# Input products of the second recurrence made beside attention, and one POOL power for three variances in the readout

## What is computed

```python
h = tok(x)                      # four 512x512 attentions per batch element -> (8, 512, 128)
xn = layernorm(layernorm(h)) * norm_g + norm_b
# first recurrence (reservoir), 256 wide, 512 steps, strictly one after the other
r_t = 0.95 * tanh(x_in_t + r_{t-1} @ W_res.T) + 0.05 * r_{t-1}
# second recurrence (linear)
delta = softplus(xn @ w_delta + b_delta);  a = exp(A * delta)
s_t = a_t * s_{t-1} + (xn @ W_B.T) * (1 - a_t) / A
read(s) = gelu(layernorm(s) @ W_ro.T + b_ro)        # s is 256 wide, the result 128
gate = sigmoid(layernorm(h) @ W_gate.T + b_gate)
h = h + read(r) * gate + read(s) * (1 - gate)
h = h + layernorm(h)            # the last stage only changes columns from 128 on, and there are 128
```

## Time and profile before

| | us |
|---|---|
| median of 3 runs (614.12 to 618.78) | 617.13 |
| profiled execution, its own time | 613.99 |
| its span | 612.1 |

### The profile page before, as it was taken

How to read it: one execution, slowest core, us unless ns; L and a number is a source line. 1 busy time by engine, 2 the same in 40 slices (tenths; PEclk the granted TensorE clock), 3 DMA queues, 4 the chain that set the end, 5 groups by cost and what they waited for, 6 DMA issues and landing times.

```text
span 612.1 us, 29176 instructions
## 1 busy us (share of the span) xinstructions
PE 571.5 (93%) x11514; PEld 469.6 (77%) x11514; DVE 524.4 (86%) x2325; ACT 430.7 (70%) x2258; POOL 202.6 (33%) x426
## 2 busy tenths in 40 slices
PE   6888787999999999999999999999999999999972
PEld 2555454788888888888888888888889988998862
DVE  6789886799888889899989999999767788899985
ACT  5587775477777777777777777777758677777764
POOL 1556464011000001110111111011100599898886
PEclk9999999899999999999999999999999999999997
DMA  6000000000000000000000000000020000000001
GB/s 219 2 2 1 2 2 1 3 4 4 4 3 4 3 4 3 4 4 4 4 4 4 4 3 3 4 3 4 3 73 2 3 20 17 20 16 20 16 19 31
DMA packets 8632, 8.35 MB, mean 14 GB/s; under 512 B 944, under 2 KB 7088, under 8 KB 8496
## 3 DMA queue, kind: packets, MB, share of 16 engines
q1 hardware_dynamic: 8208, 5.51, 3.0%
q10 hardware_dynamic: 288, 0.99, 0.5%
HBM read 3.35 MB, written 2.10 MB: 9 GB/s over the span
## 4 chain that ended last, share of the span: by engine, by line
PE 63%; POOL 23%; issue 9%; DVE 2%; DMA 1%; ACT 1%; POOLq 0%; SPq 0%; DVEq 0%
PE PS L1479 20%; PE PS L1529 15%; POOL prob_lo L448 4%; PE PS L1490 4%; POOL r_dev L516 4%; PE PS L1500 4%; POOL ln_small L526 3%; PE PS L1431 2%; PE PS L1438 2%; PE PS L1432 2%; PE PS L1494 2%; PE PS L1486 2%; POOL k L539 2%; POOL k L502 2%; POOL ln_small L530 2%
## 5 line engine op out<-in xcount | busy, mean ns | idle before, releaser
L637 ACT ACTIVATE y<-PS 128x16 f16<-128x16 f32 x512 | 94.3, 184 | 132.3 <-PE PS L1494 121.4
L1529 PE MATMUL PS<-ballast,ident 128*128 128x245 f16 (+7 forms) x648 | 142.7, 296 | 0.0
L1041 DVE TENSOR_TENSOR y_lo<-ys,y 128x16 f16<-128x16 f32 x512 | 96.5, 188 | 49.1 <-ACT ys L638 38.8
L1479 PE MATMUL PS<-y_lo,res_hi 128*128 128x8 f16 x2048 | 128.0, 168 | 2.3 <-DVE y_lo L1041 1.1
L1479 PE MATMUL PS<-y,res_hi 128*128 128x8 f16 x2048 | 127.4, 168 | 0.2
L1479 PEld LDWEIGHTS PS<-y,res_hi 128*128 128x128 f16 x2048 | 96.8, 96 | 38.8 <-ACT y L637 19.0
L1479 PE MATMUL PS<-y,res_lo 128*128 128x8 f16 x2048 | 123.4, 166 | 0.0
L453 POOL TENSOR_TENSOR small<-small,minus_half 128x2 f32<-128x2 f32 x32 | 25.6, 799 | 295.2 <-DVE y_lo L1041 260.3
L638 ACT ACTIVATE ys<-PS 128x16 f32<-128x16 f32 x512 | 99.1, 194 | 0.0
L640 ACT ACTIVATE kp<-PS 128x16 f32<-128x16 f32 x512 | 97.5, 190 | 0.0
L1479 PEld LDWEIGHTS PS<-y_lo,res_hi 128*128 128x128 f16 x2048 | 87.9, 96 | 5.5 <-DVE y_lo L1041 3.2
(11 more groups left out here) (240 smaller groups left out, 1483.8 us busy)
## 6 DMA issues: line engine op xcount, KB each, us to landing
ys<-in_x SPq DMA_DIRECT2D x8, 256.0 KB, 7.6
out<-gate_all SPq DMA_DIRECT2D x24, 64.0 KB, 1.5
mats<-in_mats ACTq DMA_DIRECT2D x1, 709.0 KB, 5.0
h_last<-h_all SPq DMA_DIRECT2D x4, 128.0 KB, 2.7
gate_last<-gate_all SPq DMA_DIRECT2D x4, 128.0 KB, 2.9
out<-gate_last SPq DMA_DIRECT2D x16, 32.0 KB, 1.9
rows<-in_rows ACTq DMA_DIRECT2D x1, 257.5 KB, 7.5
wall<-in_wall SPq DMA_DIRECT2D x1, 256.0 KB, 4.8
```

What stands on the lines that cost most here:

```text
L637: a_.activation(y16[:, :].rearrange("p (m b) -> p m b", m=NH), pre, ACT.Tanh, scale=back).then_inc(y16_ready, 1)
L1041: v.tensor_tensor(y_lo[:, :], ys[:, :, bass.ds(i * STEPS + (1 + t), 1)].rearrange("p n o -> p (n o)"), y16[:, :], ALU.subtract).then_inc(l ...
L1479: t_.matmul(dst[:, m, :], wts[:, k, m * P:m * P + P], st[:, k * B:k * B + B], start=False, stop=False, skip_group_check=True)
L1529: t_.matmul(at[:, 0:size], ident16[:, :], ballast[:, 0:size], start=False, stop=True, skip_group_check=True)
```

## The change

1. The 64 input products become 32 "drives", one per tile: two fp32 matmuls (m = 0, 1) into the last 256 columns of PSUM bank 7, made in the attention bodies. For tiles 0 to 10 they stand at t = 10 of bodies 4 to 14, for tiles 11 to 30 at t = 6 of bodies 4 to 23, for tile 31 at t = 15 of body 23. At these places `pads` returns after the drive, so the fillers of that step go. ACT copies each drive to SBUF (`take_drive`, 128x256) at t = 2 of the next body or t = 7 of the same, the last one at t = 0 of body 24.
2. `feed` is gone from PE in body 24 and after. DVE's `feed_scaled` and `recur` read and write the drives in SBUF, so that both their inputs are in SBUF.
3. The 112-column filler inside a step now also runs in bodies 25 to 31.
4. POOL takes read n-1's two variances and read n-3's layernorm variance with one addition and one power over three columns. It now waits for both (ACT's sums and DVE's `bn_aggr`) before the addition. L524 and L526 go, in the bodies; in the tail they stay as they were.
5. SP waits for the first 16 rows of the second recurrence before it moves the last quarter of h and gate, since the drives of the first quarter borrow that place.

```diff
+        last = sb("last", [P, NH, B, P])
+        h_last, gate_last = last[:, 0, :, :], last[:, 1, :, :]
+        drives = sb("drives", [P, NH, 2 * B + B // 2, P])
+        late_drives = mats[:, 0:B * P].rearrange("p (m k n) -> p m k n", m=NH, n=P)
+        DRIVE = MISC[:, 512 - NH * P:512]
...
+        FIRST_DRIVE = 4
+        LATE_DRIVE = FIRST_DRIVE + AHEAD - 2
+        def early_drive(i):
+            return i - FIRST_DRIVE if FIRST_DRIVE <= i < FIRST_DRIVE + LATE_DRIVE else None
+        def late_drive(i):
+            j = i + AHEAD - 2
+            return j if LATE_DRIVE <= j < NT - 1 else None
...
             sp.wait_ge(h_ready, NT)
+            sp.wait_ge(ssm_done, B * NH + EIGHT_FREE)
...
-                if 1 in active and u == 2:
-                    j = n - 1
-                    pool.wait_ge(r_squared, 2 * j + 2)
-                    g.tensor_tensor(r_var[:, :], r_ss[:, 1 - e, :], r_eps[:, :], ALU.add).then_inc(r_var_ready, 1)
-                    pool.wait_ge(r_var_ready, j + 1)
-                    pool.wait_ge(readout_scaled, j - 1 + TWO_FREE)
-                    g.tensor_tensor(r_dev[:, 1 - e, :], r_var[:, :], minus_half[:, :].to_broadcast([P, 2]), ALU.pow
-                                    ).then_inc(r_dev_ready, 1)
...
+                def deviations(cols, slot, added, made, count):
+                    g.tensor_tensor(var_three[:, cols], sums_read[:, slot, cols.start + 1:cols.stop + 1], eps_three[:, cols], ALU.add
+                                    ).then_inc(added, 1)
+                    pool.wait_ge(added, count)
+                    g.tensor_tensor(dev_three[:, slot, cols], var_three[:, cols],
+                                    minus_half[:, :].to_broadcast([P, cols.stop - cols.start]), ALU.pow).then_inc(made, 1)
...
+                joined = norm_last and not alone
+                if norm_last:
+                    if joined:
+                        pool.wait_ge(ln_stats, n - 2 + FREE)
+                    if n > 4:
+                        pool.wait_ge(r_out, n - 4)
+                if read_last:
+                    pool.wait_ge(r_squared, 2 * n)
+                    pool.wait_ge(readout_scaled, n - 2 + TWO_FREE)
+                    deviations(slice(0 if joined else 1, 3), 1 - e, r_var_ready, dev_made, n)
...
+            def take_drive(j):
+                act.wait_ge(drive_made, drive_count(j))
+                a_.activation(drives_of(j), DRIVE.rearrange("p (m n) -> p m n", m=NH), ACT.Copy).then_inc(drive_taken, 1)
...
             def feed_scaled(s, c):
-                dve.wait_ge(ssm_fed, c * 8 + s + 1)
-                fed = PS[:, 6 + s % 2, 0:P]
+                dve.wait_ge(drive_taken, drive_count(half_q(c) * B + c % 2 * 4 + s % 4))
+                fed = drive_row(s, c)
...
-                    v.tensor_tensor_scan(row, row, PS[:, 6 + s % 2, 0:P], first, ALU.mult, ALU.add).then_inc(ssm_done, 1)
+                    v.tensor_tensor_scan(row, row, fed, first, ALU.mult, ALU.add).then_inc(ssm_done, 1)
...
-                zeros = 112 if i < FIRST_DECAY else 0
+                zeros = 112 if i != FIRST_DECAY else 0
...
+            def drive(j):
+                b, q = j % B, j // B
+                pe.wait_ge(b_t_ready, 1)
+                if drive_count(j) > 1:
+                    pe.wait_ge(drive_taken, drive_count(j) - 1)
+                pe.wait_ge(xn_ready, j + 1)
+                for m in range(NH):
+                    one = t_.matmul(DRIVE[:, m * P:m * P + P], b_t[:, m * P:m * P + P], xn[:, b, 1 + q * P:1 + q * P + P],
+                                    start=True, stop=True, skip_group_check=True)
+                one.then_inc(drive_made, 1)
...
+                if t == 6 and late_drive(i) is not None:
+                    pe.wait_ge(gate_raw, late_drive(i) + 1)
+                    drive(late_drive(i))
+                    return
+                if t == 10 and early_drive(i) is not None:
+                    pe.wait_ge(gate_raw, j - 1)
+                    drive(early_drive(i))
+                    return
...
-                if t >= 4:
-                    feed((t - 4) % 8, (t - 4) // 8)
```

More of the change, by code:

```diff
@@ L174, in build @@
         sp_tmp = sb("sp_tmp", [P, 3, NT])
-        r_ss = sb("r_ss", [P, 2, 2])
+        sums_read = sb("sums_read", [P, 2, 4])
+        ln_mv, r_ss = sums_read[:, :, 0:2], sums_read[:, :, 2:4]
         r_mean = sb("r_mean", [P, 2, 2])
-        r_eps = sb("r_eps", [P, 2])
-        r_var = sb("r_var", [P, 2])
-        r_dev = sb("r_dev", [P, 2, 2])
+        eps_three = sb("eps_three", [P, 3])
+        var_three = sb("var_three", [P, 3])
+        dev_three = sb("dev_three", [P, 2, 3])
+        r_dev = dev_three[:, :, 1:3]
         ln_st = sb("ln_st", [P, 6])
-        ln_mv = sb("ln_mv", [P, 2, 2])
-        ln_small = sb("ln_small", [P, 2, 3])
+        ln_small = sb("ln_small", [P, 2, 2])
         ssm = keep[:, 0:SSM_LEN].rearrange("p (m q n) -> p m q n", m=NH, q=NQ + 1)
@@ L272, in build @@
         ssm_zeroed = sem("ssm_zeroed")
-        ssm_fed = sem("ssm_fed")
+        drive_made = sem("drive_made")
+        drive_taken = sem("drive_taken")
         ssm_scaled = sem("ssm_scaled")
@@ L339, in build, with drives_of, drive_count @@
         FED_EARLY = STEPS - 4
+        FIRST_DRIVE = 4
+        LATE_DRIVE = FIRST_DRIVE + AHEAD - 2
+        def drives_of(j):
+            q, b = j // B, j % B
+            if q == 0:
+                return last[:, :, b, :]
+            if j < NT - B // 2:
+                return drives[:, :, j - B, :]
+            return late_drives[:, :, b - B // 2, :]
+        def drive_count(j):
+            return 2 * j + 2 if j < LATE_DRIVE else 2 * (j - LATE_DRIVE) + 1 if j < 2 * LATE_DRIVE else j + 1
+        def early_drive(i):
[3 more added lines that the diff above has]
+            return j if LATE_DRIVE <= j < NT - 1 else None
         assert IN_SCAN == SPLIT
@@ new lines, in norm_scales @@
+                def norm_scales(slot):
+                    g.tensor_tensor(ln_small[:, slot, 0:1], dev_three[:, slot, 0:1], ones[:, 0:1], ALU.add)
+                    g.tensor_scalar(ln_small[:, slot, 1:2], ln_mv[:, slot, 0:1], dev_three[:, slot, 0:1], minus_one[:, :], ALU.mult, ALU.mult
+                                    ).then_inc(ln_dev_ready, 1)
+                read_last, norm_last = 1 in active and u == 2, 3 in active and u == 2
+                joined = norm_last and not alone
[4 more added lines that the diff above has]
+                        pool.wait_ge(r_out, n - 4)
@@ new lines, in readout @@
+                if read_last:
+                    pool.wait_ge(r_squared, 2 * n)
+                    pool.wait_ge(readout_scaled, n - 2 + TWO_FREE)
+                    deviations(slice(0 if joined else 1, 3), 1 - e, r_var_ready, dev_made, n)
+                if norm_last:
+                    if joined:
+                        pool.wait_ge(dev_made, n)
+                    else:
+                        pool.wait_ge(ln_stats, n - 2 + FREE)
+                        deviations(slice(0, 1), 1 - e, ln_var_ready, ln_pow_ready, n - IN_SCAN + 1)
+                        pool.wait_ge(ln_pow_ready, n - IN_SCAN + 1)
+                    norm_scales(1 - e)
@@ L693, in _ @@
                         gate_half(i)
+                    if t == 2 and early_drive(i - 1) is not None:
+                        take_drive(early_drive(i - 1))
+                    if t == 7 and late_drive(i) is not None:
+                        take_drive(late_drive(i))
                     if (t, i) == (7, 17):
@@ L747, in _ @@
                 scan(t, FIRST_DECAY, FIRST_DECAY % REGIONS)
+                if t == 0:
+                    take_drive(NT - 1)
                 if t >= 2:
@@ L1259, in ssm_row, with drive_row @@
                 return ssm[:, s // 4, half_q(c) + 1, (c % 2) * 4 * P + (s % 4) * P:(c % 2) * 4 * P + (s % 4) * P + P]
+            def drive_row(s, c):
+                return drives_of(half_q(c) * B + c % 2 * 4 + s % 4)[:, s // 4, :]
             def feed(s, c):
@@ L1529, in pad @@
                 t_.matmul(at[:, 0:size], ident16[:, :], ballast[:, 0:size], start=False, stop=True, skip_group_check=True)
+            def drive(j):
[8 more added lines that the diff above has]
+                one.then_inc(drive_made, 1)
             def pads(t, i):
                 j = i + AHEAD
+                if t == 6 and late_drive(i) is not None:
[6 more added lines that the diff above has]
+                    return
+                if t == 15 and j == NT:
+                    pe.wait_ge(gate_raw, NT)
+                    drive(NT - 1)
+                    return
                 tile, early, fill_at = j < NT, j <= NT, i % REGIONS < 2 and t in (4, 5, 8, 9)
@@ L1554, in pads @@
                         pe.wait_ge(gate_raw, j - 1)
+                        if late_drive(i) is not None:
+                            pe.wait_ge(drive_taken, drive_count(late_drive(i)))
                         for n in range(2 if fill_at else 4):
@@ L1745, in _ @@
```

(3 more changed lines are left out.)

42 lines of the change are left out of this document (10 added, 32 removed).

## The result

| | before | changed |
|---|---|---|
| median, us | 614.58 (6 runs, 613.78 to 618.78) | 640.14 (6 runs, 639.29 to 642.68) |
| span of the profiled execution | 612.1 | 640.9 |
| mean granted clock of it, share of full | 0.992 | 0.906 |

The changed kernel takes 1.0406 times the time of before, 95% interval 1.0371 to 1.0442: 25.6 us slower. The profiled execution is its slowest, 642.68, so the traces stand 28.8 us apart.

The account below looks back on a forecast made before the run. PE paced body 24; in the readout PE, DVE and POOL were nearly full, POOL's list as long as a read. Terms -2.4 + 2.2 - 0.6 + 0.8 + 2.0 = +2.0 us: median 619, range 610 to 627.

Parts of the forecast that it names:

- body 24, feeds gone: Body 24: 12 feeds leave PE, each step with a feed falling from 1.10 to 0.90 us; -2.4 us.
- drives on PE, attention bodies: Steps 6 and 10, attention bodies: a drive takes 0.50 us against the filler's 0.41; 0.07 x 31 = +2.2, fully exposed 2.8.
- readout, PE: Readout: feeds leave, the 112-column filler enters; PE gains some 0.1 us a read, fully only in reads 0 to 3; -0.6.
- readout, joined power: Readout, POOL's list: the second power goes, three columns cost about 0.87 us; saves 0.65 a read of POOL time.
- readout, both inputs in SBUF: Readout: DVE's two-SBUF-input instructions and POOL's block each other; +0.8 for reads 4 to 17, +2.0 for reads 18 to 27.
- tail: After the last step: same instructions, so 0.
- The new wait: Readout: POOL's addition waits for `bn_aggr` of tile n-3; loop 4.13 to 4.38 us, saving 1.8 us at the very best.
- Holds dearer: Rival, readout: two new SBUF-SBUF instructions a read lose the full 0.29 us; 14 instead of 2.8, so +13; chance 0.22.
- Floor: Rival, readout: holds fall into waits, reads come to 4.13 us; -5.1 to -7.3, 610 to 612 us; chance 0.18.
- drives hidden: Rival, attention bodies: drives cost nothing and nothing else moves; -2.4 - 0.6 = -3, 614 us; chance 0.15.
- a wait not seen at a drive: Sign of being wrong: an unseen wait at a drive, PE for `drive_taken` or ACT for `drive_made`; no size given.
- Reads at 4.2 to 4.6: Sign of being right, readout: each read still takes 4.2 to 4.6 us.

## Why the prediction was wrong, by its steps

It said 619.0 us, with 610 to 627 as its range and 0.23 for slower. It is 640.14, outside the range. (The 619.0 is +2.0 on the 617.13 that three runs gave; over six runs the kernel before is at 614.58.) The times of its steps against what was measured in the traces; the rows add up to 28.5 of the 28.8 us, the rest lies in the prologue:

| step | forecast, us | measured, us |
|---|---|---|
| body 24, feeds gone | -2.4 | -2.4 |
| drives on PE, attention bodies | +2.2 (bound 2.8) | +7.2 |
| readout, PE | -0.6 | +16.8 (the fall of the clock) |
| readout, joined power | about 0 | 0 (alone: 0.9999) |
| readout, both inputs in SBUF | +2.8 | +5.6 at full clock, of which 3.4 are shown for the scans |
| tail | 0 | +1.3, cause open |

**The step that failed is "Readout, PE".** It counted the departure of the feeds as relief (a net gain on PE of some 0.1 us a read) and no step, rival or bound asked what less matmul work does to the granted clock. That is 16.8 of 28.8 us in the traces, shown by the kernel with the work given back, and its mechanism by the one with thinner feeds. The relief itself did not come either: body 25, still at full clock, is 0.1 us shorter where 0.6 stood. The rows had a hint that I read past: the readout's windows of before stand at full clock, in a kernel that has filler products written into it, and the change took two feeds, each an fp32 matmul of 128 columns, out of each read, in a stage where most other matmuls are 8 or 16 columns wide. The range fell with it: its upper end, 627, was built from holds alone. Without this effect the changed kernel is at 624.27, +9.3 on before: inside the range, but above the likeliest case's own -2 to +6, and by other shares than forecast (the drives 7 instead of 2), so that it would have been luck.

**"Drives on PE" was mis-sized.** The mechanism was right, these matmuls are on the path of step 6 and 10. The size was not: the steps rose from 0.87 to 1.13 and to 1.07, where 0.92 to 0.95 stood in the prediction. The 0.50 was read in body 24, where nothing waits in front of the two matmuls. Here four waits do. Leaving out those that repeat another took 3.9 of the 7.1 away. So the two bounds, 0 and 0.09, were not bounds: the row came from a place without the waits, and the prediction priced only the matmuls. The 0.10 a drive that remain are close to its upper bound of 0.09, though the drive's records take 0.58 there and not 0.50; the term that was missing is the waits.

**"Body 24"** was right to the tenth; steps that took 1.10 with a feed take 0.90 to 0.91.

**"The new wait"** was right, and the most useful step: joining the powers takes some 0.65 a read out of POOL's list and turns it into POOL's wait for `bn_aggr`. Alone it moves nothing, 0.9979 to 1.0018. The loop of 4.13 to 4.38 that the prediction worked out stands beside 4.17 and 4.45 in that kernel. The three-column power was sized at 0.87; its group by line in the changed kernel (count, then busy time and mean ns of one) has 0.88:

```profile
L539 POOL TENSOR_TENSOR dev_three<-var_three,minus_half 128x3 f32<-128x3 f32 (+1 forms) x22 | 19.4, 881 | 1.7
```

**"Both inputs in SBUF"** named the right mechanism, with too small a size: 2.8 where the stage lost 5.6, of which 3.4 are shown to be the scans'. At full clock reads 4 to 17 take 4.43 (forecast 4.30) and reads 18 to 26 4.68 (forecast 4.61, from 4.41 + 0.2). Those 3.4 us come back with the scans' PSUM input; what makes the rest is open. The Trainium skill, SBUF — State Buffer, section Who interferes with whom, says that a VectorE instruction with two SBUF inputs contends with a GpSimd instruction that reads SBUF; the trace agrees, with 0.569 against 0.464 us for the scan and 0.508 against 0.455 for L527.

**The rivals.** "Holds dearer" is what the kernel with the fillers comes nearest to, but only by its total (+9.9 by its trace): its readout lost 5.6 and not 14, and the drives the rest. It is not what the changed kernel does. "Floor" and "drives hidden" are out. Of the marks at the prediction's end, POOL's idle time before the addition and the longer scans came; the busy time of POOL in the readout went from 97.8 to 89.11 in the kernel with the fillers, -8.7 where 12 was said; with the joined power alone it is 84.39, -13.4, and the two SBUF inputs, which lengthen POOL's instructions, take part of that back. The nearest of the signs of being wrong, a wait not seen at a drive, came true in a form it did not name: the 3.9 us that are shown went to waits already fulfilled. "Reads at 4.2 to 4.6" failed, and nothing in the list of marks looked at the clock.

## What to carry to other kernels

When a change takes matmuls off TensorE, or makes them narrower, in a stage where the rest are small, ask first what becomes of the granted clock there, whatever the busy share says, and put filler products in the freed places before looking for another cause. A term that was read where nothing waits in front of an instruction is no bound for a place where several waits stand. And when an engine's list is as long as the loop, look for what its shortened list will wait for before counting the cut as a gain.

## What the hardware showed that was not expected

- TensorE went from 2.4 to 1.2 GHz while it was busy 3.61 of 4.00 us, and stayed there for 109 us with 115.96 of 117.70 us busy. Being busy all the time at the lower clock did not bring the upper one back before about 609 us. The Trainium skill, TensorE: Matmul & The Clock Gate, section HAM oscillation — how this bites in real kernels, gives as its rule that TensorE should have no long idle gaps, and shows a fall during a wait for a transfer. Here PE is idle for only 0.39 us in all in the 4 us before the fall, and work given back at the same places kept the clock; so the measurement decides, and the absence of long gaps was not enough.
- One 512-column product of zeros at every second step, with the 112-column one in each step, held the clock at 1.00 for 126 us in one trace and at 0.97 in another (the drives with fewer waits); without the 112-column one it was 0.96. What the products cost doesn't show beside the +5.6 in that stage.
- Repeated waits cost TensorE time although they were fulfilled: 3.9 us of the attention bodies for 31 drives with up to four waits each, 0.13 us a drive.
- A scan with two SBUF inputs beside GpSimd's instructions takes 0.569 us on average against 0.464 with one input in PSUM and 0.475 with POOL idle, and up to 0.76.
